# A fused two-layer kernel: the context sums moved from VectorE to GpSimd, one product in its own PSUM bank in the first pairs, weight splits and small steps reordered

## The chip, the cores and the metric

One core of a Trainium2 chip runs the whole program. The metric is the device time of one execution in microseconds, lower is better. Five engines run their own programs and meet at semaphores: TensorE (PE; PEld are its weight loads), VectorE (DVE), ScalarE (ACT), GpSimd (POOL) and SyncE (SP), which issues the DMAs.

## The reference

Eight sequences of 32 tokens (256 tokens, width 512) go through two layers. Each layer is a cross-attention to 512 context rows per sequence, then a token mixer (layer 0: a gated Taylor block; layer 1: self-attention), then a feed-forward part (layer 0: a low-rank one; layer 1: experts), each added to x behind a layer norm. The change is mostly in the cross-attention:

```python
q = rms_norm((latents @ Wq).reshape(...), q_norm_w)      # 32 heads of 128
k = rms_norm((kv @ Wk).reshape(...), k_norm_w)           # 8 key heads of 128
v = (kv @ Wv).reshape(...)
scores = einsum('bhgqd,bhkd->bhgqk', qg, k) * scale      # (+ mask in layer 1)
out = einsum('bhgqk,bhkd->bhgqd', softmax(scores), v)
x = x + out.reshape(bsz, q_len, 4096) @ Wo
```

In layer 0, kv is the context with the 32 latent rows behind it; in layer 1 it is the context alone. The result is to agree in float32, so the kernel multiplies each operand as a rounded part (hi) and a rest (lo) in three matmuls.

## The kernel before

**Pairs.** The keys and values of a layer are made in 32 pairs. A unit is one sequence and one half of the key heads (4 of 8): 16 units, two pairs each (side 0 and 1, 256 context rows). Units 0 to 7 use weight half 0, units 8 to 15 half 1, and the "turn" lies between pairs 15 and 16. `quad(hf, j, b, par, cycle, u, side, m)` is called for each pair m by every engine's program. `peeled` writes out the first and the last call of each half and loops over the two in the middle, so that tests like `is_at(m, 0)` hold only in written-out pairs. `early(m)` is true for pairs 0 to 2.

**Seven products.** Each pair makes its keys and values for 256 rows by seven block products in place of eight (Strassen's scheme in Winograd's form): the context blocks A11, A12, A22 and the sums S1 to S4 against weight blocks B11, B21, B22 and the sums T1 to T4. `product` is six matmuls of 512 columns. The order on TensorE is p1, p2, p6, p5, p7, p4, p3 (list `ORDER`); p1, p6, p7 and p4 accumulate into one bank (`x_bank`), p2 has the other key bank (`y_bank`), p5 and p3 accumulate into `zbank`. ScalarE copies the growing sum out of `x_bank` after p1 (to `kn`), p6 and p7 (to `keep`) and p4. VectorE adds `y_bank` to the first keys (`ka_added`), and makes the two value blocks (`vb_added`, `va_added`) from `zbank` and `keep`.

**Attention of earlier units.** Between the products TensorE works on heads of the unit before: twice in a pair there come `p_transpose` (probabilities), `score` of a head, `kt` (keys transposed) and `pv` (probabilities by values). ScalarE's part is `pt_copy` (transposed probabilities to SBUF, `pv` waits for it), `place_k`, `exponential`, `divide`. VectorE's is `maximum`, `total` (squares summed), `normalise` (keys by their root), `tail_heads`, `lo_of_k`, `ot_place`. GpSimd makes the roots (`root`: an add and a power of 1/2 over 128x4), the queries' split (`split_queries`), the latent keys (`latent_keys`) and every fourth pair a quarter of the weight sums for later halves (`WeightSums.add`).

**Contexts.** In the first half of layer 0 the context comes in raw. The sums for pair m + 1 are made in pair m: `context.sums` (four operations of 128x256, each waiting for the one before), `contexts_hi` on ScalarE (two copies, the first waits for the third sum, the second for the fourth), `context.make_lo` on VectorE twice, and a store. Before the change, `context.sums` stands on VectorE ahead of `normalise(2 * m, 0)`, and `contexts_hi` on ScalarE ahead of the second `pt_copy`. From pair 16 of layer 0 on, the stored splits are fetched.

**Weights.** Weights of a half come as raw blocks and are split by `kvw.make_hi` (ScalarE) and `kvw.make_lo` (VectorE), 128x1024 each. At the turn this happens in pairs 15 (`turning`) and 16 (`turned`), with loads that SyncE issues as each product of pair 15 has read the place.

**Elsewhere.** `queries` opens a layer: layer norm of x, transposes, projections with a stream of weight tiles; in layer 0 `keep_busy` gives TensorE products without a use while the loads come. `Lora` is the low-rank block of layer 0; its last products wait for `l2s`, the small inner result, and for `hss`, the split sum of the hidden tiles.

Of the kernel before, what the change touches and what calls it, by code (L numbers as in the profile page):

```python
# [383 lines left out]
class Context:  # L384
# [25 lines left out]
    def sums(self, dve, b, q):  # L410
# [3 lines left out]
        dve.wait_ge(self.loaded[q], 32 * b + 32)  # L414
        for i, (out, x, y, op) in enumerate(((self.S3, self.A11, self.S1, ALU.subtract), (self.S1, self.S1, self.A22, ALU.add),
                                             (self.S2, self.S1, self.A11, ALU.subtract),
                                             (self.S4, self.A12, self.S2, ALU.subtract))):
            if i:
                dve.wait_ge(self.summed, 4 * pair + i)
            self.nc.vector.tensor_tensor(low[:, out, :], low[:, x, :], low[:, y, :], op).then_inc(self.summed, 1)  # L420
# [136 lines left out]
def queries(layer, ctx, banks, ahead=None):  # L557
# [154 lines left out]
    def tensor(pe):  # L712
# [48 lines left out]
    def scalar(act):  # L761
# [40 lines left out]
    def vector(dve):  # L802
# [56 lines left out]
        for n in range(OUTPUTS):  # L859
# [16 lines left out]
            if NL and n == CTX_SUM_AT:  # L876
                context.sums(dve, 0, 0)
# [537 lines left out]
def attend(layer, ctx, banks, border, follow=None, then=None):  # L1415
# [45 lines left out]
    ORDER = ("p1", "p2", "p6", "p5", "p7", "p4", "p3")  # L1461
    copied = s.sem("copied")
    COPIES = ("p1", "u2", "u3", "kb")
    ka_added, vb_added, va_added = s.sem("ka_added"), s.sem("vb_added"), s.sem("va_added")
# [42 lines left out]
    def made(m, name):  # L1507

        return len(ORDER) * m + ORDER.index(name) + 1

# [55 lines left out]
    def sync(sp):  # L1566
# [5 lines left out]
        def sum_weights(sp, hf, j, par, side, m):  # L1572

            if par == 0 and side == 0:
                if is_at(m, PAIRS // 2):
                    sp.wait_ge(products, made(m - 1, "p3"))
# [6 lines left out]
        def quad(hf, j, b, par, cycle, u, side, m):  # L1583
            if tail and side == 0:
# [20 lines left out]
            turn = ()  # L1605
            if is_at(m, PAIRS // 2 - 1):
                if tail:
                    wsums.all_stored(sp, 0)
                turn = zip(ORDER, range(kvw.B21, kvw.COUNT))
            for name, block in turn:  # L1610
                sp.wait_ge(products, made(m, name))
                kvw.load(sp, 1, block)
            if not is_at(u, UNITS - 1):
# [10 lines left out]
                else:  # L1624
                    sp.wait_ge(products, made(m, "p6"))
                    context.fetch(sp, nb, side, 0)
                    sp.wait_ge(products, made(m, "p3"))
# [8 lines left out]
            if is_at(m, PAIRS - 1):  # L1636
                if after is not None:
                    sp.wait_ge(products, made(m - 1, "p3"))
# [31 lines left out]
    def gpsimd(pool):  # L1670
# [34 lines left out]
        def quad(hf, j, b, par, cycle, u, side, m):  # L1705
# [10 lines left out]
            else:  # L1716
                root(2 * m, 0)
            if tail and par == 0 and side == 1:
# [12 lines left out]
    def tensor(pe):  # L1731
# [70 lines left out]
        def quad(hf, j, b, par, cycle, u, side, m):  # L1802
# [42 lines left out]
            product(hf, side, context.S3, kvw.T3, x_bank, False).then_inc(products, 1)  # L1845
            p_transpose(summed_up(u, par, side, True)[0], ka_added, m + 1, y_bank)
# [44 lines left out]
    def scalar(act):  # L1891
# [47 lines left out]
        def quad(hf, j, b, par, cycle, u, side, m):  # L1939
# [11 lines left out]
            else:  # L1951
# [19 lines left out]
            if not is_at(u, 0):  # L1971
# [13 lines left out]
            if is_at(u, 0):  # L1985
                contexts_hi(hf, b, side, m)
            else:
# [14 lines left out]
            if turning:  # L2002
                kvw.make_hi(act, 1, kvw.T1)
# [1425 lines left out]
```

## Time and profile before

| | |
|---|---|
| median of 3 runs | 1445.07 us (1444.0 to 1445.44) |
| the profiled execution | 1443.81 us, its span 1442.0 us |
| PE busy | 1414.9 us, 98% of the span |
| DVE, ACT, POOL busy | 1021.4 us (71%), 844.8 us (59%), 361.7 us (25%) |
| chain that ended last | PE 86%, DVE 7%, DMA 2%, ACT 2%, issue 2%, POOL 1% |

Busy times are those of instructions that compute; waiting isn't counted. Matmuls overlap, so a busy TensorE isn't necessarily at its peak. The chain is followed back from the last instruction, at each step to what released it. In the rows of windows below, a stretch's start and end are followed by its length, then the busy time of PE, PEld, DVE, ACT and POOL with instruction counts, the mean granted TensorE clock (1.00 is full), the DMA engines' busy share and GB/s.

### The profile page before, as it was taken

What the parts mean: (1) busy time and instruction counts of PE and PEld (TensorE: products, weight loads), DVE (VectorE), ACT (ScalarE), POOL (GpSimd) and SP (SyncE); (2) the same over time, 40 slices, a digit from 0 to 9 for tenths busy, and PEclk for the clock granted to TensorE, in tenths of its full rate; (3) what the DMA queues carried; (4) which work ended last, traced back from release to release, by engine and by line L of the source; (5) the groups of instructions that cost most, each with busy time, mean ns of one, the idle gap of its engine ahead of it and who ended that gap; (6) DMA issues with size and microseconds to landing.
All of it is one profiled execution on the core that took longest, in us unless ns stands there. A gap on an engine that the chain in (4) does not pass through costs nothing.

```text
span 1442.0 us, 24186 instructions
## 1 busy us (share of the span) xinstructions
PE 1414.9 (98%) x7942; PEld 1193.5 (83%) x7942; DVE 1021.4 (71%) x1897; ACT 844.8 (59%) x1476; POOL 361.7 (25%) x542
## 2 busy tenths in 40 slices
PE   8999999999999999999999999999999999999998
PEld 6877888887888888889778788888888888887887
DVE  7988988887666667758668555556755656776765
ACT  5845666656555556736447455556755555773443
POOL 2323323232342424015233322222221212101000
PEclk9999999999999999999999999999999999999999
DMA  7565545566455455347155433335543334342342
GB/s 274 180 234 192 189 161 186 190 220 227 142 188 169 150 163 174 117 183 229 73 178 211 153 125 126 130 118 178 166 134 121 133 123 161 132 183 68 110 159 96
DMA packets 79677, 232.44 MB, mean 161 GB/s; under 512 B 17696, under 2 KB 34848, under 8 KB 72320
## 3 DMA queue, kind: packets, MB, share of 16 engines
q1 hardware_dynamic: 79584, 231.25, 47.1%
q8 instruction: 52, 0.85, 0.2%
q14 instruction: 41, 0.34, 0.1%
HBM read 191.77 MB, written 39.45 MB: 160 GB/s over the span
## 4 chain that ended last, share of the span: by engine, by line
PE 86%; DVE 7%; DMA 2%; ACT 2%; issue 2%; POOL 1%; SPq 0%; DVEq 0%; POOLq 0%; ACTq 0%
PE g_kbanks L54 12%; PE g_kbanks L56 12%; PE g_kbanks L55 12%; PE g_pobanks L1786 8%; PE g_vbank L54 5%; PE g_vbank L55 5%; PE g_vbank L56 5%; PE g_pobanks L1772 4%; PE g_ktbank L1798 3%; PE g_sbank L1754 3%; PE g_sbank L54 2%; PE g_sbank L56 2%; PE g_sbank L55 2%; PE g_pobanks L54 1%; PE g_pobanks L56 1%
## 5 line engine op out<-in xcount | busy, mean ns | idle before, releaser
L54 PE MATMUL g_kbanks<-c_wkv_r,c_cT_r 128*128 128x512 f32 x768 | 311.4, 405 | 4.4 <-ACT c0a_keep L1984 2.1
L56 PE MATMUL g_kbanks<-c_wkv_r,c_cT_r 128*128 128x512 f32 x768 | 302.8, 394 | 0.0
L55 PE MATMUL g_kbanks<-c_wkv_r,c_cT_r 128*128 128x512 f32 x768 | 301.9, 393 | 0.0
L54 PEld LDWEIGHTS g_kbanks<-c_wkv_r,c_cT_r 128*128 128x128 f32 x768 | 144.8, 189 | 35.1 <-DVE c_wkv_r L257 2.7
L56 PEld LDWEIGHTS g_kbanks<-c_wkv_r,c_cT_r 128*128 128x128 f32 x768 | 144.2, 188 | 32.9
L55 PEld LDWEIGHTS g_kbanks<-c_wkv_r,c_cT_r 128*128 128x128 f32 x768 | 144.8, 189 | 27.2
L54 PE MATMUL g_vbank<-c_wkv_r,c_cT_r 128*128 128x512 f32 x256 | 101.1, 395 | 0.0
L55 PE MATMUL g_vbank<-c_wkv_r,c_cT_r 128*128 128x512 f32 x256 | 100.7, 393 | 0.0
L56 PE MATMUL g_vbank<-c_wkv_r,c_cT_r 128*128 128x512 f32 x256 | 100.6, 393 | 0.0
L1674 POOL TENSOR_TENSOR c1a_ms<-c1a_ss,c_const 128x4 f32<-128x4 f32 x64 | 13.7, 214 | 346.3 <-DVE c1a_ss L2101 346.3
L2107 DVE TENSOR_TENSOR c1a_kn<-c1a_kn,c1a_rstd 128x512 f32<-128x512 f32 x64 | 66.7, 1042 | 43.1 <-POOL c1a_rstd L1677 43.1
L1674 POOL TENSOR_TENSOR c0a_ms<-c0a_ss,c_const 128x4 f32<-128x4 f32 x64 | 12.9, 201 | 325.7 <-DVE c0a_ss L2101 325.7
L1923 ACT ACTIVATE c1a_pT<-g_pobanks 128x512 f32<-128x512 f32 x64 | 38.2, 597 | 88.1 <-PE g_pobanks L1772 88.0
L2107 DVE TENSOR_TENSOR c0a_kn<-c0a_kn,c0a_rstd 128x512 f32<-128x512 f32 x64 | 61.4, 960 | 34.6 <-POOL c0a_rstd L1677 34.6
L1923 ACT ACTIVATE c0a_pT<-g_pobanks 128x512 f32<-128x512 f32 x64 | 38.1, 595 | 75.2 <-PE g_pobanks L1772 75.2
L2101 DVE TENSOR_REDUCE c1a_ss<-c1a_sq 128x4 f32<-128x512 f32 x64 | 43.8, 684 | 46.6 <-ACT c1a_sq L1928 46.4
L2075 DVE CUSTOM_DVE_ANT_0 c1a_sm<-g_sbank,c_mask 128x512 f32<-128x512 f32 x64 | 44.1, 688 | 45.3 <-issue 45.2
L1786 PE MATMUL g_pobanks<-c0a_pT,c0a_v 128*128 128x128 f32 x512 | 69.3, 279 | 4.2 <-ACT c0a_pT L1923 4.0
L1786 PEld LDWEIGHTS g_pobanks<-c0a_pT,c0a_v 128*128 128x128 f32 x512 | 63.3, 194 | 6.4 <-ACT c0a_pT L1923 5.8
L1786 PE MATMUL g_pobanks<-c1a_pT,c1a_v 128*128 128x128 f32 x512 | 67.7, 275 | 0.1
L1677 POOL TENSOR_TENSOR c0a_rstd<-c0a_ms,c_const 128x4 f32<-128x4 f32 x64 | 64.8, 1012 | 5.0
L1677 POOL TENSOR_TENSOR c1a_rstd<-c1a_ms,c_const 128x4 f32<-128x4 f32 x64 | 64.6, 1009 | 5.0
(541 smaller groups left out, 3776.2 us busy)
## 6 DMA issues: line engine op xcount, KB each, us to landing
c_cT_r<-ctx_split_dram SPq DMA_DIRECT2D x48, 1024.0 KB, 5.7
c_cT_r<-ctx_split_dram SPq DMA_DIRECT2D x48, 768.0 KB, 4.8
ctx_split_dram<-c_cT_r SPq DMA_DIRECT2D x16, 1792.0 KB, 6.5
c_wkv<-in_l_wo SPq DMA_DIRECT2D x16, 1024.0 KB, 4.9
g_stage<-in_l_wq SPq DMA_DIRECT2D x15, 1024.0 KB, 5.1
e_stage<-in_e_w SPq DMA_DIRECT2D x20, 768.0 KB, 4.2
c_cT<-in_ctx SPq DMA_DIRECT2D x32, 256.0 KB, 3.0
m_stage<-in_mix_ffn SPq DMA_DIRECT2D x10, 768.0 KB, 4.3
```

The lines of the kernel that those rows point to most:

```text
L54: nc.tensor.matmul(out, a[0], b[1], start=start, stop=False, skip_group_check=reopen)
L55: nc.tensor.matmul(out, a[0], b[0], start=False, stop=False, skip_group_check=reopen)
L56: return nc.tensor.matmul(out, a[1], b[0], start=False, stop=stop, skip_group_check=reopen)
L1677: nc.gpsimd.tensor_tensor(rstd[:, k, :], ms[:, k, :], const[:, 0, :], ALU.pow).then_inc(k_rstd, 1)
L1754: last = nc.tensor.matmul(sbank[:, side * CTX:side * CTX + HALF], q[qp][:, apar, k, :], kT[kp][:, apar, k, side * HALF:(side + 1) * HALF], ...
L1772: last = nc.tensor.transpose(ptbank[:, t * P:(t + 1) * P], p[:, t * P:(t + 1) * P], ident[:])
L1786: last = nc.tensor.matmul(obank[:, 0:P], v[:, apar, t, k * HD:(k + 1) * HD], pT[:, t, :], start=(t == 0), stop=(t == CT - 1 and not tail))
L1798: last = nc.tensor.transpose(ktbank[:, h * P:(h + 1) * P], kn[:, k, h * P:(h + 1) * P], ident[:])
L1923: nc.scalar.activation(pT[:, :, :], ptbank[:, :].rearrange("p (t n) -> p t n", t=CT), ACT.Copy).then_inc(pt_ready, 1)
L2075: nc.vector.tensor_tensor_reduce(out=sm[:], in0=sbank[:, 0:CTX], in1=mask[:], scale=-1.0, scalar=3.4e38, op0=ALU.add, op1=ALU.min, accum_o ...
L2101: nc.vector.tensor_reduce(ss[:, k, :], sq[:, :].rearrange("p (h d) -> p h d", h=UNIT_H), AX.X, ALU.add).then_inc(k_summed, 1)
L2107: nc.vector.tensor_tensor(heads, heads, rstd[:, k, :].unsqueeze(2).broadcast_to([P, UNIT_H, HD]), ALU.mult).then_inc(k_normed, 1)
```

## The change

- `context.sums` takes the engine as an argument. In pairs 0 to 2 (those with `early(m)`) VectorE still makes the sums, now behind `normalise(2 * m, 0)`, and ScalarE's `contexts_hi` moves behind the second exponential. In pairs 3 to 14 GpSimd makes them, behind `root(2 * m, 0)` and, on side 1, `split_queries` and `latent_keys`.
- In the pairs of unit 0 (0 and 1, both layers) the seventh product p3 runs between p7 and p4 into `obank`, and VectorE makes `va` in two additions. `FIRST` is the order there.
- Early pairs: the square of the first keys moves ahead of the copy after p6. Layer 1: an exponential of four columns in pair 0.
- Turn: SyncE loads B21 first; the splits of B21 and T2 come later in pair 15, T1, T3, T4 and B22 in pair 16, and T2's rest is made in pair 16.
- Start: one warm product fewer, x normalised and split ahead of parts of the weight split.
- `Lora`: the parts of the last down products that need only `hs_hi` run before the small product; one of two small ScalarE copies is made by VectorE.

```diff
@@ queries: tensor, scalar, vector
             pe.wait_ge(warm_set, 1)
-            keep_busy(UW, 3)
+            keep_busy(UW, 2)
...
-        for t in range(TT):
-            if first:
-                for c in (2 * t, 2 * t + 1):
-                    stream.make_first_hi(act, c)
-            ln.make_hi(act, t)
+        if first:
+            stream.make_first_hi(act, 0)
+            ln.make_hi(act, 0)
+            for c in range(1, DC):
+                stream.make_first_hi(act, c)
+            ln.make_hi(act, 1)
...
             ln.moments(dve, 0)
+            ln.normalise(dve, 0)
             stream.make_first_lo(dve, 0)
-            ln.normalise(dve, 0)
+            ln.make_lo(dve, 0)
             stream.make_first_lo(dve, 1)
-            ln.make_lo(dve, 0)
@@ attend: sync, quad
+            turning = is_at(m, PAIRS // 2 - 1)
+            if turning:
+                if tail:
+                    wsums.all_stored(sp, 0)
+                sp.wait_ge(products, made(m, "p1"))
+                kvw.load(sp, 1, kvw.B21)
             if tail and side == 0:
...
+            if turning:
+                for name, block in zip(ORDER[1:], range(kvw.T2, kvw.COUNT)):
+                    sp.wait_ge(products, made(m, name))
+                    kvw.load(sp, 1, block)
@@ attend: gpsimd, quad
             else:
                 root(2 * m, 0)
+            if prepared(hf, m + 1) and not early(m):
+                pool.wait_ge(products, all_made(m - 1))
+                context.sums(pool, nc.gpsimd, *following(hf, b, side))
             if tail and par == 0 and side == 1:
@@ attend: tensor, quad
             product(hf, side, context.S3, kvw.T3, x_bank, False).then_inc(products, 1)
+            if is_at(u, 0):
+                wait_weights(kvw.B22)
+                if is_at(m, 0):
+                    pe.wait_ge(*border.placed)
+                product(hf, side, context.S4, kvw.B22, obank, True).then_inc(products, 1)
...
-            wait_weights(kvw.B22)
-            pe.wait_ge(vb_added, m + 1)
-            product(hf, side, context.S4, kvw.B22, zbank, False).then_inc(products, 1)
+            if not is_at(u, 0):
+                wait_weights(kvw.B22)
+                pe.wait_ge(vb_added, m + 1)
+                product(hf, side, context.S4, kvw.B22, zbank, False).then_inc(products, 1)
@@ attend: scalar, quad
                 if turned:
-                    kvw.make_hi(act, 1, kvw.T4)
+                    kvw.make_hi(act, 1, kvw.T1)
                 pt_copy(summed_up(u, par, side, False)[0])
             if not early(m):
...
                 exponential(x1, k1)
+                if turned:
+                    kvw.make_hi(act, 1, kvw.T3)
+            if early(m):
+                key_square(2 * m, 0, ka_added, m + 1)
             act.wait_ge(products, made(m, "p6"))
...
             if early(m):
-                key_square(2 * m, 0, ka_added, m + 1)
+                if is_at(m, 0) and not tail:
+                    act.wait_ge(const_set, 2)
+                    nc.scalar.activation(p[:, 0:UNIT_H], const[:, 0, :], ACT.Exp)
...
             divide(x1, k1)
-            if not is_at(u, 0):
+            if not early(m):
                 contexts_hi(hf, b, side, m)
...
-            if turning:
-                kvw.make_hi(act, 1, kvw.B21)
             if turned:
+                kvw.make_hi(act, 1, kvw.T4)
                 kvw.make_hi(act, 1, kvw.B22)
             pt_copy(summed_up(u, par, side, True)[0])
...
             exponential(x2, k2)
+            if early(m):
+                contexts_hi(hf, b, side, m)
             if turning:
-                kvw.make_hi(act, 1, kvw.T2)
+                kvw.make_hi(act, 1, kvw.B21)
...
             divide(x2, k2)
             if turning:
-                kvw.make_hi(act, 1, kvw.T1)
-                kvw.make_hi(act, 1, kvw.T3)
+                kvw.make_hi(act, 1, kvw.T2)
@@ attend: vector, quad
+            if turned:
+                kvw.make_lo(dve, 1, kvw.T2)
             dve.wait_ge(copied, kept(m, "p1"))
...
+            normalise(2 * m, 0)
             if prepared(hf, m + 1):
-                if not is_at(m, 0):
-                    dve.wait_ge(products, made(m - 1, "p3"))
-                context.sums(dve, *following(hf, b, side))
-            normalise(2 * m, 0)
-            if prepared(hf, m + 1) and not is_at(u, 0):
-                context.make_lo(dve, *following(hf, b, side), 0)
+                if early(m):
+                    if not is_at(m, 0):
+                        dve.wait_ge(products, all_made(m - 1))
+                    context.sums(dve, nc.vector, *following(hf, b, side))
+                else:
+                    context.make_lo(dve, *following(hf, b, side), 0)
...
+            if is_at(u, 0):
+                dve.wait_ge(products, made(m, "p5"))
+                nc.vector.tensor_tensor(keep[:, 0, :], zbank[:, :], keep[:, 0, :], ALU.add).then_inc(va_part, 1)
+                dve.wait_ge(va_part, m + 1)
+                dve.wait_ge(products, made(m, "p3"))
+                nc.vector.tensor_tensor(v[:, par, 2 * side, :], obank, keep[:, 0, :], ALU.add).then_inc(va_added, 1)
@@ Lora: tensor, scalar
+        m = LORA_M - 1
+        pe.wait_ge(self.hs_hi, LORA_M)
+        for t in range(TT):
+            for w in reversed(self.dw):
+                nc.tensor.matmul(self.ybank[t][:, :], self.hss[0][:, m, t * P:(t + 1) * P], w[:, m, :],
+                                 start=False, stop=False)
         pe.wait_ge(self.l2_hi, 2)
...
-        for i in range(2):
-            nc.scalar.activation(self.l2s[i * QUAD:i * QUAD + LORA_R, :], self.lbank[0:LORA_R, 0:TOK], ACT.Copy,
-                                 scale=0.5).then_inc(self.l2_hi, 1)
+        nc.scalar.activation(self.l2s[0:LORA_R, :], self.lbank[0:LORA_R, 0:TOK], ACT.Copy,
+                             scale=0.5).then_inc(self.l2_hi, 1)
```

## Rows read from the trace of the kernel before

**Rows 1.** The page's first part: busy time of each engine.

```profile
PE 1414.9 (98%) x7942; PEld 1193.5 (83%) x7942; DVE 1021.4 (71%) x1897; ACT 844.8 (59%) x1476; POOL 361.7 (25%) x542
```

**Rows 2.** Waits of TensorE: who ended them, us in total, times, longest.

```profile
PE g_pobanks L1786 <- ACT c0a_pT L1923: 4.0, 1, 4.0
PE g_kbanks L54 <- ACT c0a_keep L1984: 2.1, 3, 0.8
...
PE g_kbanks L54 <- ACT c1a_keep L1984: 1.5, 2, 0.8
PE g_pobanks L1000 <- DVE c0q_xn L994: 1.4, 2, 1.1
PE g_kbanks L2763 <- ACT f_l2s L2807: 1.4, 1, 1.4
...
PE g_ktbank L1798 <- DVE c1a_kn L2107: 0.8, 2, 0.6
```

**Rows 3.** Windows: pairs 9, 10, 15, 16 (layer 0), 16 (layer 1), and behind the gap.

```profile
217.87:233.77 15.90, 15.80 (x91) 13.28 (x90) 14.78 (x28) 10.17 (x20) 9.39 (x12) 1.00 0.44 161
233.77:249.06 15.29, 15.29 (x91) 13.19 (x90) 13.06 (x28) 10.21 (x20) 2.42 (x4) 1.00 0.53 193
311.11:332.27 21.16, 17.13 (x91) 14.65 (x90) 14.27 (x25) 11.32 (x21) 5.81 (x8) 0.92 0.84 274
332.27:348.42 16.15, 15.67 (x91) 13.14 (x90) 13.75 (x25) 12.18 (x22) 2.42 (x4) 1.00 0.77 262
1013.33:1028.72 15.39, 15.11 (x82) 12.32 (x80) 12.33 (x24) 11.90 (x22) 2.42 (x4) 1.00 0.59 201
...
326.70:330.90 4.20, 4.12 (x16) 3.71 (x17) 3.75 (x10) 2.75 (x6) 0.00 (x0) 0.59 0.77 246
```

**Rows 4.** Timeline of POOL, sides 1 and 0, and a later pair: start, us.

```profile
224.39 1.01 POOL L1677 TENSOR_TENSOR c0a_rstd<-c0a_ms,c_const 128x4 f32<-128x4 f32 x1
...
227.39 0.55 POOL L1702 TENSOR_TENSOR g_stage_r<-c_klat,c0a_kT_hi 128x128 fp32r<-128x128 f32 x1
227.90 4.22 POOL L309 TENSOR_TENSOR c_wkv<-c_wkv 128x256 f32<-128x256 f32 x4
...
240.23 1.01 POOL L1677 TENSOR_TENSOR c0a_rstd<-c0a_ms,c_const 128x4 f32<-128x4 f32 x1
...
358.57 6.31 POOL L309 TENSOR_TENSOR c_wkv<-c_wkv 128x256 f32<-128x256 f32 x8
```

**Rows 5.** Timeline of ACT over the same two pairs.

```profile
227.19 1.80 ACT L428 ACTIVATE c_cT_r<-c_cT 128x768 fp32r<-128x768 f32 x2 [0.95 <-DVE c_cT L420]
228.89 0.58 ACT L1923 ACTIVATE c0a_pT<-g_pobanks 128x512 f32<-128x512 f32 x1
...
242.06 1.80 ACT L428 ACTIVATE c_cT_r<-c_cT 128x768 fp32r<-128x768 f32 x2
```

**Rows 6.** Timeline of PE over the same two pairs: the second pv.

```profile
229.52 1.16 PE L1786 MATMUL g_pobanks<-c0a_pT,c0a_v 128*128 128x128 f32 x8
...
245.25 1.06 PE L1786 MATMUL g_pobanks<-c0a_pT,c0a_v 128*128 128x128 f32 x8
```

**Rows 7.** Timeline of DVE: the side-0 pair, then pair 1.

```profile
240.70 1.80 DVE L420 TENSOR_TENSOR c_cT<-c_cT 128x256 f32<-128x256 f32 x4
...
105.08 3.20 DVE L420 TENSOR_TENSOR c_cT<-c_cT 128x256 f32<-128x256 f32 x4
...
109.50 2.98 DVE L434 TENSOR_TENSOR c_cT_r<-c_cT,c_cT_r 128x768 fp32r<-128x768 f32 x2
```

**Rows 8.** Timeline at the turn of layer 0: ACT, PE, DVE.

```profile
325.18 1.06 ACT L248 ACTIVATE c_wkv_r<-c_wkv 128x1024 fp32r<-128x1024 f32 x1 [5.70 <-DMA c_wkv<-in_l_wkv]
...
341.38 0.50 PE L54 MATMUL g_kbanks<-c_wkv_r,c_cT_r 128*128 128x512 f32 x1 [0.48 <-DVE c_wkv_r L257]
...
341.85 2.35 DVE L257 TENSOR_TENSOR c_wkv_r<-c_wkv,c_wkv_r 128x1024 fp32r<-128x1024 f32 x2
```

**Rows 9.** Timeline of ACT in pair 2 of layer 1.

```profile
821.29 1.28 ACT L1909 ACT_TABLE_LOAD   x1
```

More of the change, by code:

```diff
@@ L418, in sums @@
             if i:
-                dve.wait_ge(self.summed, 4 * pair + i)
-            self.nc.vector.tensor_tensor(low[:, out, :], low[:, x, :], low[:, y, :], op).then_inc(self.summed, 1)
+                eng.wait_ge(self.summed, 4 * pair + i)
+            engine.tensor_tensor(low[:, out, :], low[:, x, :], low[:, y, :], op).then_inc(self.summed, 1)
     def piece(self, ap, q, i, half):
@@ L876, in vector @@
             if NL and n == CTX_SUM_AT:
-                context.sums(dve, 0, 0)
+                context.sums(dve, nc.vector, 0, 0)
             for i, at in enumerate(LO_AT):
@@ L1507, in made, with all_made @@
     def made(m, name):
-        return len(ORDER) * m + ORDER.index(name) + 1
+        order = FIRST if is_at(m, 0) or is_at(m, 1) else ORDER
+        return len(order) * m + order.index(name) + 1
+    def all_made(m):
+        return len(ORDER) * (m + 1)
     def kept(m, name):
@@ L1604, in quad @@
                 kvw.load(sp, 1, kvw.B11)
[L1605 to L1612, printed above, removed]
+            if turning:
+                for name, block in zip(ORDER[1:], range(kvw.T2, kvw.COUNT)):
+                    sp.wait_ge(products, made(m, name))
+                    kvw.load(sp, 1, block)
             if not is_at(u, UNITS - 1):
@@ L1984, in quad @@
             nc.scalar.activation(keep[:, 1, :], x_bank, ACT.Copy).then_inc(copied, 1)
-            if is_at(u, 0):
-                contexts_hi(hf, b, side, m)
-            else:
+            if not is_at(u, 0):
                 place_k(2 * m, 2 * side, par, u)
             exponential(x2, k2)
+            if early(m):
+                contexts_hi(hf, b, side, m)
             if turning:
-                kvw.make_hi(act, 1, kvw.T2)
+                kvw.make_hi(act, 1, kvw.B21)
             if last:
@@ L2159, in quad @@
             nc.vector.tensor_tensor(v[:, par, 2 * side + 1, :], zbank[:, :], keep[:, 1, :], ALU.add).then_inc(vb_added, 1)
-            if prepared(hf, m + 1) and is_at(u, 0):
-                context.make_lo(dve, *following(hf, b, side), 0)
             if not is_at(u, 0):
@@ L2168, in quad @@
             if turning:
-                kvw.make_lo(dve, 1, kvw.T2)
+                kvw.make_lo(dve, 1, kvw.B21)
             if prepared(hf, m + 1):
-                context.make_lo(dve, *following(hf, b, side), 1)
+                if early(m):
+                    context.make_lo(dve, *following(hf, b, side), 0)
+                if not is_at(m, 1):
+                    context.make_lo(dve, *following(hf, b, side), 1)
             if last:
@@ L2175, in quad @@
             total(2 * m + 1, 1)
+            if prepared(hf, m + 1) and is_at(m, 1):
+                context.make_lo(dve, *following(hf, b, side), 1)
             if is_at(u, 0):
@@ L2179, in quad @@
                 lo_of_k(2 * m, 2 * side, par)
-            dve.wait_ge(products, made(m, "p3"))
             dve.wait_ge(copied, kept(m, "u2"))
-            nc.vector.tensor_tensor(v[:, par, 2 * side, :], zbank[:, :], keep[:, 0, :], ALU.add).then_inc(va_added, 1)
+            if is_at(u, 0):
[4 more added lines that the diff above has]
+                nc.vector.tensor_tensor(v[:, par, 2 * side, :], obank, keep[:, 0, :], ALU.add).then_inc(va_added, 1)
+            else:
+                dve.wait_ge(products, made(m, "p3"))
+                nc.vector.tensor_tensor(v[:, par, 2 * side, :], zbank[:, :], keep[:, 0, :], ALU.add).then_inc(va_added, 1)
             if last:
@@ L2763, in tensor @@
             nc.tensor.matmul(self.ybank[t][:, :], self.l2s[:, t * P:(t + 1) * P], self.b2s[:], start=False, stop=False)
-        m = LORA_M - 1
-        pe.wait_ge(self.hs_lo, LORA_M)
-        for t in range(TT):
-            mm3(nc, self.ybank[t][:, :], tuple(v[:, m, t * P:(t + 1) * P] for v in self.hss),
-                tuple(w[:, m, :] for w in self.dw), False, True).then_inc(self.y_done, 1)
+            if t == 0:
+                pe.wait_ge(self.hs_lo, LORA_M)
+            nc.tensor.matmul(self.ybank[t][:, :], self.hss[1][:, m, t * P:(t + 1) * P], self.dw[0][:, m, :],
+                             start=False, stop=True).then_inc(self.y_done, 1)
     def scalar(self, act, mix, next_tile):
```

20 lines of the change are left out of this document (12 added, 8 removed).

## The prediction

> **What bounds the kernel now.** I read the page's first part, the waits of TensorE, the windows of single pairs, and then the timelines of four engines over two neighbouring pairs. TensorE is busy for 1414.9 us of the 1442.0 us span [rows 1], so its gaps add up to 27 us, and no reordering that leaves the matmuls alone can win more than that, plus the slow clock behind a gap. The waits say where they lie [rows 2]: one of 4.0 us at the change of halves in layer 0, several of 0.6 to 0.8 us in the first three pairs of each layer, one of 1.4 us at the end of the low-rank block, and 1.4 us in two pieces at the start. Between these places TensorE doesn't wait: a pair takes 15.9 us with side 1 and 15.3 with side 0, and PE is busy for 15.80 and 15.29 of them [rows 3]. So the question has two halves: what the edits win at those places, and whether anything that they add reaches TensorE in a pair that is full now.
>
> **The costly part: context sums on GpSimd, in pairs 3 to 14.** Follow one pair m in the new order. GpSimd first does the root of its keys' norm, `root(2m, 0)`; only behind it, and in a side-1 pair behind `split_queries` and `latent_keys` too, come the four sums. ScalarE's `contexts_hi` waits for the third and the fourth sum, and in its program the second `pt_copy` of the pair stands directly behind it. On that copy TensorE's second `pv` waits, with the fourth and seventh products of the pair queued behind it.
>
> Now the times. In the side-1 pair the root ends at 224.39 + 1.01 = 225.40 and `latent_keys` at 227.39 + 0.55 = 227.94; in the side-0 pair the root ends at 240.23 + 1.01 = 241.24 [rows 4]. These are the earliest starts of the sums. GpSimd has the same operation, 128x256 with both inputs in SBUF, in `WeightSums.add`: eight in 6.31 us when VectorE leaves it alone, so 0.79 each, and four in 4.22, so 1.06 each, when VectorE runs its own sums [rows 4]. In the new order VectorE stands still during the sums, since its `make_lo` of the context waits for ScalarE's copy, so I take 0.80 each. The third sum then ends at 230.3 (side 1) and 243.6 (side 0), the fourth at 231.1 and 244.4. ScalarE's two copies take 1.80 together, and the next instruction starts 1.70 behind the first of them [rows 5]; the second copy can't begin before the fourth sum, so 231.1 and 244.5, and `pt_copy` starts about 0.95 later, 232.1 and 245.4, and takes 0.6. The second `pv` starts at 232.75 in place of 229.52, and at 246.1 in place of 245.25 [rows 6]. With 0.1 for the restart of an idle engine that is 3.3 us in a side-1 pair and 0.95 in a side-0 pair. Six pairs of each: 6 x 3.3 + 6 x 0.95 = 25.5 us.
>
> Does the loss recur, or is it paid once? The chain from the second product through the keys' sum, square, total, root, sums, copies and back to `pv` starts and ends on TensorE inside the same pair. A late pair starts the next chain just as late, so it recurs. And the relief? VectorE gives up 1.80 us a pair [rows 7], but it then waits for the copies, and TensorE didn't wait for VectorE in these pairs. I count it at nothing. Behind the sums on GpSimd stand `wsums.add` in every fourth pair and then the root of the second keys; `wsums.add` would end at 235.3, before that root's input is there in a pair so much longer, so they cost nothing. If the sums on GpSimd were slowed to 1.06 each, 12 x 3 x 0.26 = 9 us more would be due; that is the upper end of this term, and 20 us the lower, if the queries' split and the hand-over are a little quicker than I read them.
>
> One more cost hangs on it, the clock. After the 4.0 us gap TensorE ran 4.20 us at a granted 0.59, so half its speed for most of that [rows 3]; 4.20 x 0.41 = 1.7 us lost. Behind gaps of up to 1.4 us nothing of the kind shows. A gap of 3.3 lies between, nearer to 4.0. Six of them cost 0 to 10 us. One row of 4.0 doesn't say that every such gap does it, and ours are shorter, so I take two falls, 3.4 us.
>
> The SBUF rule of the Trainium skill speaks against this edit as well ("SBUF — State Buffer", section "SBUF: two separate sides"): a VectorE operation with two SBUF inputs and a GpSimd operation take a shared port pair as a lock, so one blocks for the other's whole instruction. The trace agrees, with four VectorE sums in 1.80 us alone and in 3.20 beside GpSimd [rows 7]. By that rule alone moving the sums would free VectorE of less than the 1.80; the sum here gives it no gain in either case.
>
> **The change of halves.** In layer 0 ScalarE waits in pair 15 for the load of B21 (5.70 us, until 325.18) with the second `pt_copy` behind it [rows 8]. The diff puts that split behind the second exponential and sends its load ahead of three small ones on SP's queue, which start 0.8 us later and are read only in the next unit. The copy then waits for its transposes alone. Gone are the 4.0 us and the 1.7 of slow clock: 21.16 against 15.3 for a full-speed pair [rows 3]. What is late next: pair 16 gets the split of T2 on VectorE on top of four others, all before its second half. One split costs 1.2 (2.35 for two), and TensorE waits 0.48 us for such a split there already [rows 8], so I charge 1.1. Net -4.6, between -6 and -3. In layer 1 the same pair 15 has no such gap, so nothing is won, and pair 16, now 15.39 [rows 3], gets the same extra split: +1.0, between 0 and +2.
>
> **The first pairs.** The seventh product goes to its own bank between the fifth and the sixth, and covers the copy of the keep buffer that TensorE waits for in pairs 0 and 1 (0.8 each with the restart) [rows 2]. In layer 1 that holds: 1.6 us. There the table load of 1.28 us in front of the first exponential [rows 9] moves to an idle moment in pair 0 as well, and the keys' waits behind it (0.8) [rows 2] go, with 0.4 more from the earlier square: -2.8, between -1.5 and -3.5. The extra VectorE addition (0.7) stands where the engine is free. In layer 0 VectorE is the late one. In pair 1 it makes the sums in 3.20 us from 105.08, and the first of the two splits behind them, begun at 109.50 and half of 2.98 long, ends at 111.0, just as the next pair's first product starts [rows 7]. The new order puts the sums behind a normalisation, which waits 1.0 us for GpSimd's power and more, so they begin some 1.7 later, and so does pair 2; the 0.8 won in pair 0 comes off. +1.0, between -1.5 and +3.
>
> **Start and low-rank block.** With x normalised ahead of the weight split (0.7) and one warm product less, the first projection can start 1.2 earlier, if the weights' loads allow; the 1.4 us of waits at that place bound it [rows 2]. -1.2, between -1.5 and 0. At the end of the low-rank block four of the last products no longer wait for the small result, and one ScalarE copy goes to VectorE. TensorE's 1.4 us wait shrinks, but the outcome is tied to VectorE's rest of the split sum behind it: -0.4, between -1 and 0.
>
> **Sum.** 25.5 + 3.4 - 4.6 + 1.0 + 1.0 - 2.8 - 1.2 - 0.4 = +21.9. On the profiled execution's own 1443.81 us (span 1442.0) that makes 1465.7; the median of the runs lies 1.3 above it, so 1467.
>
> **Rivals.** (1) The sums are hidden: `pt_copy` is not held up. The edits elsewhere stay: -7.0 without the first two terms, 1438, faster. It would need the second context copy to begin at 227.9 in a side-1 pair and at 242.8 in a side-0 pair, its place now [rows 5], so the fourth sum would have to end 3.2 and 1.6 earlier than above; that is the point from which it decides. For it speaks only that GpSimd is idle for most of a pair; against it, that the idle time lies before the root. Chance 0.08. (2) The stall is shorter, as the sums start or run quicker than their kin (20 us at most, no fall of the clock), and the won places pay in full (-13): about 1452. Chance 0.12. (3) The clock falls behind every long gap: 6 x 1.7 in place of 3.4, and the sums take 1.06 each: 1467 + 6.8 + 9 = 1483. That an idle stretch takes the clock to half is what the Trainium skill says too ("TensorE: Matmul & The Clock Gate", section "Why this matters for your kernels"), and the row of 0.59 agrees with it; each of the six gaps would then be followed by a stretch at 1.2 GHz. Chance 0.12. My forecast, 0.68, spans 1457 to 1476.
>
> **How the numbers follow.** A measurement of this kernel tells about 0.2% (2.9 us) from nothing. Faster is rival 1 and a little of the tail of 2, 0.09; within 0.2%, 0.03; slower, 0.88. The range leaves out rival 1 and part of the ends of 2 and 3: 1452 to 1480.
>
> **What the profile will show.** If I am right: 48 sums on POOL at the context's tile, beginning right behind the root or `latent_keys`; idle time of ScalarE before the context copies put down to POOL; waits of the second `pv` for `pT` of about 3.3 and 1 us in turn; pairs 3 to 14 of some 19 and 16 us in turn; no 4 us gap at the change of halves in layer 0; layer 1 shorter by about 2 us. If the sums' start isn't tied to the root, or the copies' wait isn't ahead of `pt_copy`, the pairs keep their 15.3 and 15.9 and rival 1 holds. The prediction is also wrong if GpSimd's sum takes 0.6 or 1.5 in this company, or if the clock behaves as in rival 3.

## The result and the profile after

The changed kernel takes 1470.95 us (median of 4 runs, 1470.05 to 1472.69) against 1444.53 for the one before: ratio 1.0181, 95% interval 1.0165 to 1.0198. It is slower, as forecast, and 4 us above the 1467 of the forecast. The profiled execution has a span of 1469.7 us, 27.7 more than before.

The page's first part, which answers to [rows 1]:

```profile
PE 1421.1 (97%) x7940; PEld 1197.5 (81%) x7940; DVE 1008.7 (69%) x1854; ACT 845.2 (58%) x1476; POOL 397.3 (27%) x590
```

TensorE's busy time grew by 6.2 us with two matmuls fewer (one warm product less). The slow clock, 7.4 us as shown below, is enough to account for that, and the rest of the 27.7 is waiting. The waits of TensorE say where, as [rows 2] did before (who ended them, us in total, times, longest):

```profile
PE g_pobanks L1802 <- ACT c0a_pT L1945: 25.9, 12, 3.9
PE g_kbanks L54 <- DVE c_cT_r L434: 3.5, 3, 2.7
```

There are twelve waits of `pv` for the transposed probabilities, one for each pair from 3 to 14, in place of the single one at the change of halves. The timelines of GpSimd, ScalarE and TensorE in pairs 9 and 10 of the changed kernel show the chain (start, us, instruction, idle time before it and who ended it):

```profile
242.94 1.01 POOL L1690 TENSOR_TENSOR c0a_rstd<-c0a_ms,c_const 128x4 f32<-128x4 f32 x1
...
246.01 0.46 POOL L1715 TENSOR_TENSOR g_stage_r<-c_klat,c0a_kT_hi 128x128 fp32r<-128x128 f32 x1
246.43 3.14 POOL L420 TENSOR_TENSOR c_cT<-c_cT 128x256 f32<-128x256 f32 x4
...
262.54 3.52 POOL L420 TENSOR_TENSOR c_cT<-c_cT 128x256 f32<-128x256 f32 x4
```

```profile
248.80 1.86 ACT L428 ACTIVATE c_cT_r<-c_cT 128x768 fp32r<-128x768 f32 x2 [4.01 <-POOL c_cT L420]
250.56 0.58 ACT L1945 ACTIVATE c0a_pT<-g_pobanks 128x512 f32<-128x512 f32 x1
...
265.27 1.88 ACT L428 ACTIVATE c_cT_r<-c_cT 128x768 fp32r<-128x768 f32 x2 [1.79 <-POOL c_cT L420]
```

```profile
251.19 1.16 PE L1802 MATMUL g_pobanks<-c0a_pT,c0a_v 128*128 128x128 f32 x8 [3.15 <-ACT c0a_pT L1945]
...
267.69 1.16 PE L1802 MATMUL g_pobanks<-c0a_pT,c0a_v 128*128 128x128 f32 x8 [0.95 <-ACT c0a_pT L1945]
```

Read them downwards for the side-1 pair. The root ends at 243.95, the latent keys at 246.47, the four sums at 249.57. ScalarE stood 4.01 us in front of the context copies, and `pt_copy` starts at 250.56 although its transposes had ended 3.7 us earlier. From the root's end to `pv` it is 7.24 us; the forecast had 7.35 (225.40 to 232.75). In side 0 VectorE's normalisation runs beside the sums, which take 3.52 in place of 3.14. The windows of the same two pairs, as in [rows 3]:

```profile
236.40:255.10 18.70, 15.55 (x91) 13.23 (x90) 13.24 (x24) 10.25 (x20) 11.77 (x16) 1.00 0.38 137
255.10:271.59 16.49, 15.54 (x91) 13.22 (x90) 12.07 (x24) 10.26 (x20) 5.69 (x8) 1.00 0.48 179
```

The side-1 pair grew from 15.90 to 18.70, so by 2.80 and not by the whole 3.15; the side-0 pair grew from 15.29 to 16.49, by 1.20 and not by 0.95. Both fit one sum: a pair without waits takes 15.29, a stall costs its listed wait and some 0.25 more, and the 0.6 us by which the side-1 pair was longer before the change are gone in the long wait (15.29 + 3.15 + 0.26 = 18.70).

**The account.** The same instruction's start is taken in both traces (in the second and the sixth row less the wait in front of it), and the offsets are subtracted from each other. The marks of the third row thus take in pair 3's wait, 3.95 us, and all that follow.

| stretch | marks (before, after) | forecast | measured |
|---|---|---|---|
| start and queries of layer 0 | first product of pair 0: 87.08, 86.44 | -1.2 | -0.6 |
| first pairs of layer 0 | second `pv` of pair 3: 136.64, 137.24 without its wait | +1.0 | +1.2 |
| pairs 3 to 14 | second `pv` of pair 14: 307.30, 341.46 | +28.9 | +33.6 |
| change of halves, layer 0 | first low-rank product: 700.07, 730.24 | -4.6 | -4.0 |
| low-rank block | first transposes of layer 1: 734.34, 764.21 | -0.4 | -0.3 |
| opening and first pairs of layer 1 | waiting product of pair 16: 1021.81, 1048.51 | -2.8 | -3.2 |
| change of halves, layer 1 | last expert product: 1437.12, 1464.76 | +1.0 | +0.9 |

The sum is 27.6. Of the 33.6 in the third row, 7.4 are slow clock (below), so the stall itself is 26.2 where the forecast had 25.5. In pair 3 the chain is no longer than in pair 9 (the root ends at 133.96, `pv` starts 7.23 later), but TensorE would have come to `pv` 3.3 us behind the root there and not 4.1, so that wait is 0.8 us longer than the others.

### The profile page after: what moved, and what is told of

Same layout as the page of the kernel before. It is cut to its first block, busy times and chain, and to the rows that moved or that the text cites. A ratio compares the mean times of both kernels' runs of the same rounds, so it can differ in the third digit from the quotient of the medians.

```text
span 1469.7 us, 24205 instructions
## 1 busy us (share of the span) xinstructions
PE 1421.1 (97%) x7940; PEld 1197.5 (81%) x7940; DVE 1008.7 (69%) x1854; ACT 845.2 (58%) x1476; POOL 397.3 (27%) x590
## 4 chain that ended last, share of the span: by engine, by line
PE 82%; DVE 7%; POOL 4%; issue 2%; ACT 2%; DMA 2%; POOLq 0%; ACTq 0%; DVEq 0%; SPq 0%
PE g_kbanks L54 12%; PE g_kbanks L56 11%; PE g_kbanks L55 11%; PE g_pobanks L1802 7%; PE g_vbank L54 5%; PE g_vbank L56 5%; PE g_vbank L55 5%; PE g_pobanks L1788 3%; PE g_ktbank L1814 3%; PE g_sbank L1770 2%; PE g_sbank L54 2%; PE g_sbank L55 2%; PE g_sbank L56 2%; PE g_pobanks L54 2%; PE g_pobanks L56 1%
## 5 line engine op out<-in xcount | busy, mean ns | idle before, releaser
L54 PE MATMUL g_vbank<-c_wkv_r,c_cT_r 128*128 128x512 f32 x248 | 99.2, 400 | 1.6 <-DVE c0a_v L2186 0.9
L2133 DVE TENSOR_TENSOR c0a_kn<-c0a_kn,c0a_rstd 128x512 f32<-128x512 f32 x64 | 69.9, 1092 | 41.8 <-POOL c0a_rstd L1690 41.8
L56 PE MATMUL g_vbank<-c_wkv_r,c_cT_r 128*128 128x512 f32 x248 | 97.9, 395 | 0.0
L55 PE MATMUL g_vbank<-c_wkv_r,c_cT_r 128*128 128x512 f32 x248 | 97.8, 394 | 0.0
L2127 DVE TENSOR_REDUCE c0a_ss<-c0a_sq 128x4 f32<-128x512 f32 x64 | 43.9, 685 | 34.0 <-ACT c0a_sq L1950 32.2
```

Source lines behind the costliest of these rows:

```text
L54: nc.tensor.matmul(out, a[0], b[1], start=start, stop=False, skip_group_check=reopen)
L55: nc.tensor.matmul(out, a[0], b[0], start=False, stop=False, skip_group_check=reopen)
L56: return nc.tensor.matmul(out, a[1], b[0], start=False, stop=stop, skip_group_check=reopen)
L2127: nc.vector.tensor_reduce(ss[:, k, :], sq[:, :].rearrange("p (h d) -> p h d", h=UNIT_H), AX.X, ALU.add).then_inc(k_summed, 1)
L2133: nc.vector.tensor_tensor(heads, heads, rstd[:, k, :].unsqueeze(2).broadcast_to([P, UNIT_H, HD]), ALU.mult).then_inc(k_normed, 1)
```

## The experiments

Each was timed in alternation with the kernel before (1445.0 to 1445.7 in these sessions). "The head version" is the kernel of run e3_sums_first.

**e1_sums_vector: everything but the engine of the sums.**

```diff
 # vector, quad
+            if prepared(hf, m + 1) and not early(m):
+                dve.wait_ge(products, all_made(m - 1))
+                context.sums(dve, nc.vector, *following(hf, b, side))
             normalise(2 * m, 0)
 # gpsimd, quad
-            if prepared(hf, m + 1) and not early(m):
-                pool.wait_ge(products, all_made(m - 1))
-                context.sums(pool, nc.gpsimd, *following(hf, b, side))
```

> The changed kernel with the sums of pairs 3 to 14 back on VectorE, ahead of normalise(2 * m, 0), where they stood before; every other edit stays. Forecast's theory: between pairs 3 and 14 the changed kernel loses 33.4 us (its second pv of pair 14 stands 34.2 behind that of before, and its pair 3 only 0.8), all of it by the sums on GpSimd, so this one takes 1471.0 - 33.4 = 1437.6 us, with no wait of the second pv for pT and pairs of 15.9 and 15.3. Rival (another edit of these pairs, or the slower clock in general, makes part of the loss): some long waits of pv stay and the time is over 1445.

Measured: 1438.08 us, ratio to before 0.9950 (0.9933 to 0.9967). That is the forecast's theory (1437.6). No wait for `pT` over 0.32 us is left. The whole loss hangs on this one edit; all the others together win 7.3 us, where the forecast's terms sum to -7.0.

**e4_before_gpsimd_sums: that edit alone, on the kernel before.** The sums move to GpSimd behind `root(2 * m, 0)`, or behind `latent_keys` in side 1; nothing else changes.

> The kernel before with one edit: the sums of pairs 3 to 14 on GpSimd behind the root (and split_queries, latent_keys), as the changed kernel has them. Theory 1 (the loss is the sums' alone): waits of the second pv for pT of 3.2 and 1.0 us in turn, 26 us in all, and three to six falls of the clock behind the long ones: 1444.5 + 33 = 1478, between 1475 and 1481. Rival (the loss needs the other edits too, such as the order of normalise and sums): under 1470.

Measured: 1476.38 us, 1.0218 (1.0201 to 1.0235), with waits of 3.16 to 3.30 and 0.92 to 1.05 us in turn: theory 1 (1475 to 1481). The loss needs nothing else.

**e2_copies_late: the same late sums, but `pt_copy` no longer queued behind the copies.**

```diff
 # scalar, quad
             divide(x1, k1)
-            if not early(m):
-                contexts_hi(hf, b, side, m)
...
             exponential(x2, k2)
-            if early(m):
-                contexts_hi(hf, b, side, m)
+            contexts_hi(hf, b, side, m)
```

On VectorE both `make_lo` of the context stand behind the second `ot_place` in every pair.

> The changed kernel with the sums left on GpSimd where they are, but with contexts_hi behind the second exponential in every pair (as the change has it in pairs 0 to 2) and both make_lo behind the second ot_place. Theory 1 (the sums hurt only because pt_copy stands behind the copies that wait for them): the waits of pv for pT are gone, copies and splits still end before the next pair, 1438 to 1441. Theory 2 (the sums end too late for the next pair in any order): the wait moves to the first product of the next pair, which then waits for the context's rest, over 1 us in side-1 pairs, and the time is 1445 to 1460. Theory 3 (GpSimd's sums slow VectorE so that pairs lengthen without a wait of pv): over 1460.

Measured: 1438.95 us, 0.9955 (0.9938 to 0.9971). In its pair 9 ScalarE's timeline reads:

```profile
229.36 0.60 ACT L1945 ACTIVATE c0a_pT<-g_pobanks 128x512 f32<-128x512 f32 x1 [2.07 <-PE g_pobanks L1788]
...
231.92 1.89 ACT L428 ACTIVATE c_cT_r<-c_cT 128x768 fp32r<-128x768 f32 x2
```

and GpSimd's sums start as late in the pair as in the changed kernel (229.53, taking 3.18). So theory 1 holds: the sums were in time for the next pair. The changed kernel loses 32 us to this one because an instruction that needed the sums stood in ScalarE's program ahead of one that didn't. The late sums aren't free here either: from the second `pv` of pair 3 to that of pair 14 this kernel takes 172.5 us (137.07 to 309.54), the kernel before 170.7. Of that, a wait of `kt` of 0.6 to 0.7 us in three pairs behind `WeightSums.add` is listed.

**e6_sums_behind_root: the sums 2.5 us earlier in side-1 pairs**, directly behind the root and ahead of the queries' rest and the latent keys.

> The changed kernel with the four sums of a side-1 pair directly behind the root, ahead of the rest of the queries' split and the latent keys (which end 2.5 us later in the forecast's rows); side 0 unchanged. Theory 1 (the wait of pv is the start of the sums plus fixed times): the waits of 3.15 us become 0.6 to 1.0, like those of side 0, the clock doesn't fall any more, so 6 x 2.4 and 7.6 us of slow clock less than 1471: 1449. Rival (the long waits come from a slower sum beside VectorE's work, not from the start): waits of over 2 us stay and the time is over 1458.

Measured: 1454.27 us, 1.0060 (1.0043 to 1.0077), between the two expectations. The waits:

```profile
PE g_pobanks L1806 <- ACT c0a_pT L1949: 13.2, 12, 1.8
```

and the window of pair 9 (pair 10 takes 16.49, as in the changed kernel):

```profile
228.43:245.39 16.96, 15.80 (x91) 13.31 (x90) 13.05 (x24) 10.26 (x20) 11.85 (x16) 1.00 0.41 151
```

The mechanism of theory 1 holds (eleven of the twelve waits are 0.95 to 1.2 us, as in side 0), its price doesn't. The side-1 pair shrank by 1.74, where the expectation had 2.4: the listed wait by 2.1, less 0.4 of short waits that the long one had covered. And the clock fell once behind the 1.81 us wait in pair 3 (1.4 us) and once in the low-rank block (1.3 us). 6 x 1.74 and 7.4 - 1.4 - 1.3 are 15.1, which is the difference of the two spans, 1469.7 and 1454.6.

**e3_sums_first: the sums ahead of the root.**

```diff
 # gpsimd, quad
             if not is_at(m, 0):
                 root(2 * m - 1, 1)
+            if prepared(hf, m + 1) and not early(m):
+                pool.wait_ge(products, all_made(m - 1))
+                context.sums(pool, nc.gpsimd, *following(hf, b, side))
             if is_at(m, 1):
                 root(2 * m, 0)
...
-            if prepared(hf, m + 1) and not early(m):
-                pool.wait_ge(products, all_made(m - 1))
-                context.sums(pool, nc.gpsimd, *following(hf, b, side))
```

> The changed kernel with GpSimd's four sums ahead of root(2 * m, 0), split_queries and latent_keys in pairs 3 to 14, directly behind root(2 * m - 1, 1); ScalarE and VectorE as in the changed kernel. Theory 1 (the place behind the root costs the time, the engine itself doesn't): the sums end some 6 us into the pair, ahead of the copies' turn, no stall, 1437 to 1440. Theory 2 (the sums, 3.5 us, now delay the root of the first keys, which normalise and kt wait for): kt waits about 1 us in each of 12 pairs, 1445 to 1452. Theory 3 (on the shared SBUF access VectorE's own operations lengthen with GpSimd's): pairs of over 16.2 without one clear wait, over 1445.

Measured: 1434.59 us, 0.9927 (0.9911 to 0.9944): theory 1 in its mechanism, faster than its 1437 to 1440, and 3.5 us better than with the sums on VectorE. GpSimd and the windows of pairs 9 and 10 in its trace:

```profile
219.16 3.70 POOL L420 TENSOR_TENSOR c_cT<-c_cT 128x256 f32<-128x256 f32 x4
...
223.86 1.02 POOL L1690 TENSOR_TENSOR c0a_rstd<-c0a_ms,c_const 128x4 f32<-128x4 f32 x1
```

```profile
216.97:232.26 15.29, 15.29 (x91) 13.18 (x90) 13.05 (x24) 10.27 (x20) 12.37 (x16) 1.00 0.45 167
232.26:247.53 15.27, 15.27 (x91) 13.20 (x90) 11.47 (x23) 10.17 (x20) 5.90 (x8) 1.00 0.53 193
```

In the side-1 pair the root's first operation now starts at 223.58, 0.5 us behind its input, where it was 0.1 before, and nobody on TensorE waits for it. The side-1 pair is now as short as the side-0 pair: 15.29 against 15.90 in [rows 3].

**e11_before_sums_first: does VectorE's relief pay by itself?** It has the same place for the sums, as the only edit of the kernel before.

> The kernel before with one edit: the sums of pairs 3 to 14 at the head of GpSimd's part. Theory 1 (VectorE's sums cost the kernel before 0.3 to 0.65 us in each side-1 pair in waits too short to be listed; those pairs' halves of 8.44 to 8.79 and 7.14 become 8.34 and 6.94): 1444.9 - 3.2 = 1441.7. Rival (the forecast's: relief of VectorE is worth nothing, and the gain of the like change on the changed kernel came from elsewhere): 1444.5 to 1445.5.

Measured: 1442.78 us, 0.9979 (0.9970 to 0.9989), 2.6 less than before and between the two expectations. Its window of pair 9 (pair 10 takes 15.29, as before):

```profile
216.27:231.54 15.27, 15.27 (x91) 13.20 (x90) 13.48 (x24) 10.17 (x20) 12.13 (x16) 1.00 0.45 168
```

From the second `pv` of pair 3 to that of pair 14 it takes 168.1 us (136.06 to 304.14) against 170.7 before (136.64 to 307.30), and pair 3's own is in neither. The profiled execution has two slow-clock stretches that the kernel before doesn't have or has shorter (the one behind the 3.97 us wait at the change of halves, and one of some 3 us in the low-rank block), so its span is only 1.0 us shorter. So the relief is real, 0.3 to 0.65 us in each side-1 pair, and the forecast's "I count it at nothing" is wrong.

TensorE's waits there are too short to be listed (gaps under 0.15 us). They are found by laying the starts of the same matmuls in pairs 9 and 10 of the kernel before beside each other: the two pairs run alike up to the second `pv`, which is 0.17 us late in pair 9, and the matmul behind it (L1790), which needs VectorE's small stack of the latent rows' probabilities, is 0.60 late. Three rows of pair 9 before the change, VectorE's and TensorE's:

```profile
224.85 2.76 DVE L420 TENSOR_TENSOR c_cT<-c_cT 128x256 f32<-128x256 f32 x4
...
230.43 0.28 DVE L2087 TENSOR_TENSOR c0a_pT_stack<-g_kbanks,c0a_pT_stack 32x128 fp32r<-32x128 f32 x1
...
230.76 0.33 PE L1790 MATMUL g_pobanks<-c0a_pT_stack,c_vlat 96*128 96x128 f32 x1
```

The stack is ready at 230.71 and TensorE takes it at 230.76. VectorE's four sums and the split behind them run beside GpSimd's work in this pair and take 2.76 and 1.50 us, against 1.80 and 0.95 in pair 10, so it is here that they hold up what stands behind them.

**e7_turn_only: the change of halves alone, on the kernel before.**

> The kernel before with the turn's edits alone (B21's load first, later splits). Theory 1 (the turn's terms stand by themselves): layer 0's wait of 4.0 us and the slow clock behind it gone, new waits of 0.7 and 0.9 in pair 16, layer 1's turn 0.9 us longer: net -4.0 + 0.9, 1441.5. Rival (the win in the changed kernel came from ScalarE or VectorE running later against TensorE in the pairs ahead): the 4.0 us wait stays in part, 1443 to 1446.

Measured: 1440.65 us, 0.9970 (0.9958 to 0.9983). The 4.0 us wait is gone, and the new waits in pair 16 (0.74 and 0.90 in layer 0, 0.92 in layer 1) are those of the changed kernel to 0.01 us. Theory 1 holds: the terms stand by themselves.

**e5_all_on_gpsimd: the head version with pairs 0 to 2 on GpSimd too.**

> The kernel with the sums at the head of GpSimd's part (the run before of that name), now in pairs 0 to 2 too; VectorE makes none. In the changed kernel VectorE's sums in pair 1 take 3.44 us from 106.06 and the first product of pair 2 waits 2.66 us for the split behind them. Theory 1 (VectorE is late there with the sums): that wait and those of 0.9 and 0.4 in pair 2 are gone, 3 to 4 us less than 1434.6, so 1431. Theory 2 (the raw context is there so late, or the copies on ScalarE stand so late, that the split ends late whoever sums): the wait stays over 1.5 us and the time is 1433 to 1436.

Measured: 1434.31 us, no different from e3's 1434.59. The wait of pair 2's first product is gone, but another took its place:

```profile
PE g_ktbank L1815 <- DVE c0a_kn L2134: 3.0, 2, 2.7
```

In pair 1 GpSimd's `WeightSums.add` runs from 107.96 to 112.0; the root of that pair's second keys, whose sum of squares was there at 109.1, comes behind it, and `kt` of pair 2 waits. Neither theory had this wait.

**e9_first_pairs_on_gpsimd: those weight sums moved behind pair 2's context sums**, and layer 1's turn as before.

> The kernel with all sums at the head of GpSimd's part, with the splits at the turn of layer 1 as before, and with the weight sums of pair 1 (4.06 us on GpSimd, from 107.96) moved behind pair 2's context sums. Theory 1 (the 2.74 us wait of kt in pair 2 comes from the root of pair 1's second keys queued behind those weight sums): that wait falls under 0.5, and with 0.9 of the turn of layer 1 and 1.7 of slow clock behind the long wait the time is 1434.3 - 2.5 - 0.9 - 1.7 = 1429.2, 1431 if the clock falls anyway. Rival (GpSimd's work is only shifted, root(4, 0) is late now): kt waits over 1.5 us in pair 2 and the time is over 1432.

Measured: 1434.83 us, 0.9929 (0.9912 to 0.9946): the rival. `kt` waits 0.94 and 3.12 us; the weight sums run until 118.5, and now it is the root of pair 2's first keys that stands behind them. The granted clock is at 0.50 for 5.6 us behind the wait. In both places that were tried in these pairs, 3 us of weight sums ahead of a root hold it up.

**e10_early_sums_ahead: VectorE's sums of pairs 0 to 2 ahead of the normalisation**, on the head version, with layer 1's turn as before.

```diff
 # vector, quad
+            if prepared(hf, m + 1) and early(m):
+                if not is_at(m, 0):
+                    dve.wait_ge(products, all_made(m - 1))
+                context.sums(dve, nc.vector, *following(hf, b, side))
             normalise(2 * m, 0)
```

> The kernel with the sums at the head of GpSimd's part in pairs 3 to 14 and layer 1's turn as before; in pairs 0 to 2 of layer 0 the new order of products stays, and only VectorE's sums go back ahead of normalise(2 * m, 0). Theory 1 (as forecast: the sums behind the normalisation make pair 2 late): the 2.66 us wait of the first product of pair 2 shrinks by 1 or more, 1434.6 - 0.9 - 1.2 = 1432.5. Rival (not their place but the copies behind the second exponential and the extra addition hold the split up): the wait stays at 2.2 to 2.7 and the time is 1433.7.

Measured: 1433.07 us, 0.9915 (0.9899 to 0.9932). The sums of pair 1 start at 104.02 in place of 106.06, and the wait of pair 2's first product is 1.17 in place of 2.66 us; part of it comes back as a wait of `kt` (1.06). The time lies between the two expectations, which the runs can't tell apart; the wait speaks for theory 1.

**e8_old_first_l0_old_turn_l1: two places put back.** The head version, with layer 0's pairs 0 to 2 and layer 1's splits at the turn as in the kernel before (conditions on `tail`).

> The kernel with the sums at the head of GpSimd's part, with two places put back as they were before: pairs 0 to 2 of layer 0 (order of products, of the sums, the copies and the square) and the splits at the turn of layer 1. Theory 1 (by the offsets between the two traces these cost 1.4 and 0.9 us): 1434.6 - 2.3 = 1432.3. Rival (they cost only beside the late sums): 1434 to 1436.

Measured: 1432.50 us (1432.24 to 1433.39), 0.9914 (0.9897 to 0.9930). Theory 1, and the fastest kernel of the study, 38 us below the changed kernel.

**e12_turn_l0_reordered: VectorE's order in pair 16.**

> The kernel of 1432.5 us (sums at the head of GpSimd's part, layer 0's first pairs and layer 1's turn as before) with VectorE's order in pair 16 of layer 0 changed: the rest of T1 ahead of the first maximum, that of T3 directly behind it, the sum's inverse next, then the rest as it was; ScalarE splits T3 right behind the first pt_copy. Theory 1 (TensorE's waits of 0.75 and 0.90 us in pair 16 are VectorE's queue order, as in the forecast's term of 1.1 for this pair): both shrink, 1.2 us in sum, 1431.3. Rival (VectorE is simply full in this pair, and whatever is put back later is waited for as long, kt or the second transposes): 1432 to 1433.

Measured: 1433.36 us, 0.9923 (0.9910 to 0.9937), no faster. The waits of 0.75 and 0.90 us are gone, and in their place TensorE waits 0.37 for ScalarE's copy to `keep` and, in the same pair:

```profile
PE g_pobanks L1806 <- DVE c0a_pT_stack L2121: 1.3, 1, 1.3
```

That is the rival: with five splits of 1.2 us VectorE is full here (in the trace of e8 it works without a listed pause from the pair's start until 339.1, 12 us), and what is put back is waited for.

## Why the prediction was right

**The stall: right, in mechanism and size.** Sums behind the root, ScalarE's copy behind the sums, `pt_copy` behind the copy, `pv` behind that: waits of 3.15 and 0.95 us measured against 3.3 and 0.95. That the total (26.2 against 25.5) agrees so closely is in part luck: a side-1 pair grew by less than its wait, a side-0 pair by more, and pair 3 waited 0.8 us longer than the others. e1 and e4 show that the edit alone makes the loss, e2 that ScalarE's order is the link that passes it on, e3 and e6 that the start of the sums sets its size. The argument that the stall recurs in each pair held: none of the twelve waits is missing. Rivals 1 and 2 are out.

**The clock: right that it falls, one term too small.** Behind the six long waits of the changed kernel the granted clock fell four times, not twice. These are windows of the 4.00 us behind the waits in pairs 7 and 9:

```profile
214.37:218.37 4.00, 4.00 (x16) 3.43 (x17) 3.57 (x7) 1.73 (x5) 0.00 (x0) 0.63 0.00 0
251.19:255.19 4.00, 4.00 (x22) 3.45 (x23) 3.92 (x9) 2.99 (x7) 1.94 (x3) 1.00 0.02 2
```

Both follow waits of 3.13 and 3.15 us. The next first `pv` comes 10.00 us behind the one and 8.45 behind the other, so a fall to the lower level (0.50, 1.2 GHz) costs 1.55; behind pair 3's wait of 3.95 it took 11.15, which is 2.7. Together 2.7 + 3 x 1.55 = 7.4 in place of 3.4. This is the mis-sized term: 4.0 of the 5.7 us between the account's 27.6 and the forecast's sum of 21.9. The medians are only 4 us apart because the forecast added 1.3 for the step from the profiled execution to the median, while the changed kernel's profiled execution (1471.46) stood 0.5 above its median; that is luck. The term lies between the forecast and rival 3, which had all six. The Trainium skill ("TensorE: Matmul & The Clock Gate", section "Why this matters for your kernels") warns that idle stretches between bursts of matmuls bring the slow clock back. The rows agree that they can, and show besides that two waits of the same length in the same place of the program may go either way.

**VectorE's relief: the step that was wrong**, though in the changed kernel it is hidden in the stall. "It then waits for the copies, and TensorE didn't wait for VectorE in these pairs" overlooked the 0.6 us between the two windows of [rows 3], whose matmul counts are equal; busy time hid it, since it was 15.80 in the one and 15.29 in the other for the same matmuls. And what VectorE gives up in the side-1 pair 9 is 2.76 us, not the 1.80 of the side-0 row. Where the sums are in time it is worth 2.6 us (e11 against before) to 3.5 us (e3 against e1).

**The sums' length: close.** 0.80 each was taken; they took 3.14 for four in side 1 and 3.52 in side 0, since VectorE did have something to run beside them, the normalisation. That slowed too: it takes 1.23 us beside the sums in pair 6 of the changed kernel where 0.69 is its time alone, which agrees with the lock that the Trainium skill describes ("SBUF — State Buffer", section "SBUF: two separate sides"). In side 0 the overlap wasn't free: the sums stand in the chain that `pv` waits for, and there they took 0.38 us longer than in side 1. The row from which the forecast took its slow rate, 1.06 each "when VectorE runs its own sums", was misread: the weight sums of 4.22 us began at 227.90, and VectorE's sums had ended at 227.61; what ran beside them were the end of a normalisation and a split.

**The other places.** Turn of layer 0: -4.0 against -4.6, the new waits in pair 16 being 1.6 us where 1.1 was charged. Turn of layer 1: +0.9 against +1.0. First pairs: +1.2 and -3.2 against +1.0 and -2.8; e10 shows the cause given for layer 0, the sums behind the normalisation, to be half of the 2.66 us wait in pair 2. What makes the rest (the later copies or the extra addition) wasn't separated. Start: -0.6 against -1.2; the first product of pair 0 stands between 85.9 and 86.6 in the ten traces with this edit and between 86.5 and 87.1 in the four without, so its size is hardly above its scatter. Low-rank block: -0.3 against -0.4, and no run takes it apart.

## What to carry to other kernels

Moving work to an idle engine is judged by where it stands in that engine's program and by what stands behind its consumer in the consumer's program, not by the engine's idle share. The same four sums on the same engine cost 33 us behind the root and won 3 ahead of it. In a full pipeline compare windows of like stages with equal matmul counts: a difference of half a microsecond can be a wait that neither the list of waits nor the busy share shows, and the starts of the same matmuls, laid beside each other, say where it is.

## What wasn't expected of the hardware

The granted clock is not a function of the wait in front of it. Over the traces here it fell behind waits of 1.81 us (e6), 2.65 (e1) and 2.74 (e5), but not behind 2.66 us at e1's product in the changed kernel, e2, e3 and e6; of the waits of 3.13 to 3.32 us in the changed kernel and e4 it fell behind seven and not behind four. In the low-rank block, where three waits of 0.5 to 0.6 us stand within 6 us, it fell for some 3 us in four traces (e5, e6, e10, e11) and in the other ten not at all, at a price of 1.3 us each. So a difference of 1.3 or 1.6 us between two of these profiles can be the clock alone. What decides between two equal waits stays open.
